# A transformer decoder layer: the quantised feed-forward restructured, and the last batch of the attention layers kept in one piece

## The reference

```python
def _act_fake_quant(x, clip_factor):
    scale = jax.nn.sigmoid(clip_factor) * jnp.max(jnp.abs(x)) / QMAX
    return jnp.clip(_ste_round(x / scale), -QMAX - 1.0, QMAX) * scale
...
xq = _act_fake_quant(x, clip_x[0])
gate = jnp.einsum('bsh,ih->bsi', xq, _weight_fake_quant(w_gate))
up = jnp.einsum('bsh,ih->bsi', xq, _weight_fake_quant(w_up))
h = _act_fake_quant(jax.nn.silu(gate) * up, clip_down[0])
return jnp.einsum('bsi,hi->bsh', h, _weight_fake_quant(w_down))
```

## Time and profile before

| | |
|---|---|
| median of 3 runs | 1102.18 us (1100.94 to 1102.88) |
| the profiled execution's own time | 1098.88 us |
| its span in the profile | 1097.1 us |
| busy in the span: PE | 917.2 us (84%) |
| DVE | 734.1 us (67%) |
| ACT | 628.8 us (57%) |
| POOL | 355.2 us (32%) |
| mean granted TensorE clock | 0.921 of full speed |

### The profile page before, as it was taken

The page is one execution under the profiler, slowest core; times in us unless marked ns, Lnnn a source line. Parts: engine busy times, 40 slices in busy tenths (PEclk is TensorE's granted clock), DMA queues, the critical chain, the costliest instruction groups (busy, mean ns, idle before and its releaser), DMA issues. The chain is left out here.

```text
span 1097.1 us, 17747 instructions
## 1 busy us (share of the span) xinstructions
PE 917.2 (84%) x5861; PEld 439.7 (40%) x5865; DVE 734.1 (67%) x1566; ACT 628.8 (57%) x1173; POOL 355.2 (32%) x381
## 2 busy tenths in 40 slices
PE   2898999999999997999999887899986884458454
PEld 1443334554445353444453643333443443123222
DVE  6588876677776548786763666878744665376574
ACT  1335777567686733577867345576562443488562
POOL 6821156205311173143025643111033210134223
PEclk9989999999999998999999999999997677688667
DMA  4341172201311321122123113211123112111043
GB/s 146 100 119 51 59 87 64 60 30 52 99 58 39 116 77 57 40 75 90 32 73 107 49 59 98 91 61 45 54 78 113 55 50 80 55 57 58 0 153 115
DMA packets 82600, 79.60 MB, mean 73 GB/s; under 512 B 19560, under 2 KB 76008, under 8 KB 82520
## 3 DMA queue, kind: packets, MB, share of 16 engines
q1 hardware_dynamic: 77384, 75.03, 22.2%
q10 hardware_dynamic: 3456, 2.94, 0.8%
q0 software_dynamic: 1680, 0.58, 0.6%
HBM read 23.48 MB, written 14.18 MB: 34 GB/s over the span
## 5 line engine op out<-in xcount | busy, mean ns | idle before, releaser
L672 ACT ACTIVATE probs<-psum 128x512 f32<-128x512 f32 (+1 forms) x608 | 312.8, 579 | 157.4 <-PE psum L862 154.4
L1027 DVE CUSTOM_DVE_ANT_0 junk<-psum,mask 128x640 bf16<-128x640 f32 (+3 forms) x256 | 252.5, 1022 | 60.6 <-PE psum L827 58.7
L592 POOL TENSOR_SCALAR_AFFINE_SELECT probs<-probs 128x512 f32<-128x512 f32 x128 | 82.2, 645 | 372.2 <-ACT probs L672 372.1
L862 PE MATMUL psum<-q_stack,k_stack 98*128 98x512 bf16 (+3 forms) x768 | 186.8, 331 | 14.7 <-ACT probs L672 5.5
L887 PE MATMUL psum<-probs,v_sb 128*17 128x512 f32 (+3 forms) x1536 | 158.8, 493 | 1.8 <-POOL probs L592 1.6
L827 PE MATMUL psum<-k_stack,q_stack 96*128 96x512 bf16 (+3 forms) x512 | 130.1, 349 | 12.9 <-DVE rowmax L1027 9.1
L862 PEld LDWEIGHTS psum<-q_stack,k_stack 98*128 98x128 bf16 x768 | 62.1, 97 | 149.8 <-ACT probs L672 95.1
L1023 DVE TENSOR_REDUCE rowmax<-psum 128x4 f32<-128x512 f32 (+2 forms) x96 | 97.1, 1044 | 35.5 <-PE psum L821 35.3
L787 PE MATMUL psum<-xnT,wT 128*128 128x512 f32 x192 | 94.3, 625 | 0.4 <-ACT probs L672 0.3
L714 PE MATMUL psum<-wT,xnT 128*128 128x256 f32 x384 | 89.3, 390 | 1.7 <-ACT xnT L640 1.5
L677 ACT ACTIVATE xprobs<-psum 77x512 f32<-77x512 f32 x128 | 67.6, 590 | 29.0 <-PE psum L871 28.7
(11 more groups left out here) (152 smaller groups left out, 1310.0 us busy)
## 6 DMA issues: line engine op xcount, KB each, us to landing
k_stack<-k_parts SPq DMA_DIRECT2D x216, 64.0 KB, 2.6
q_stack<-q_parts SPq DMA_DIRECT2D x192, 64.0 KB, 2.6
xq_stack<-xq_parts SPq DMA_DIRECT2D x192, 64.0 KB, 2.6
xn<-in_x SPq DMA_DIRECT2D x8, 512.0 KB, 6.3
res<-in_x SPq DMA_DIRECT2D x4, 1024.0 KB, 6.4
resid_hbm<-res SPq DMA_DIRECT2D x8, 512.0 KB, 2.6
normT_hbm<-xnT SPq DMA_DIRECT2D x8, 512.0 KB, 7.1
xf<-normT_hbm SPq DMA_DIRECT2D x8, 512.0 KB, 4.2
```

The lines of the kernel that those rows point to most:

```text
L592: nc.gpsimd.affine_select(out=tile, in_=tile, compare_op=ALU.is_ge, fill=0.0, base=0, pattern=[[0, GH], [1, P]], channel_multiplier=-1).th ...
L672: nc.scalar.activation(probs[n % 2][:, heads * k:heads * k + heads, 0:cols], bank_a(s)[:, 0:heads * cols].rearrange("p (h n) -> p h n", h= ...
L862: last = nc.tensor.matmul(bank[:, cols * n:cols * n + cols], k_stack[:, slot, h, P * j:P * j + P], q_stack[:, slot, half, h, q0 - HALF * h ...
L1027: nc.vector.tensor_tensor_reduce(out=junk[D_STEPS.place(s) % 2][:, 0:keys], in0=bank_d(s)[:, 0:keys], in1=m.mask[:, T - keys:T], scale=1.0 ...
```

## The change

**The layers.** The last batch is no longer split: parts(b) gives (BOTH,) for all batches, and lane y is empty. The last batch has no tstore; the tile xnT, which holds its feed-forward input, now lives on into the feed-forward. PICKS is new throughout. In it the query and key projections of batches 2 and 3 stand ahead of the last softmax steps of the batch before (at most 33 and 30 softmax steps follow the first of them); in the old one they stand behind the last of them.

**The feed-forward.** All loops are unrolled, and the last batch's two blocks come first, read from xnT.

- partition_all_reduce is gone. TensorE turns the column of maxima into a row (a transpose), VectorE reduces the row, and TensorE spreads the result (a product with ones).
- GpSimd rounds x (one instruction of 128x1024), three blocks ahead of the tiles.
- All tiles have 128 rows (the weights are padded with zeros). VectorE multiplies tiles 0 to 2, GpSimd tiles 3 to 5, whose up ScalarE copies out.
- VectorE takes one maximum a block over 3072 elements, one block behind; the last block's in two pieces.
- ScalarE rounds a whole block of hidden values in one instruction (3072 elements) and takes the constant off four of the six slices in a second; VectorE takes it off the other two, and clips the block in one instruction, 3072 elements, with both bounds.
- The down projection has four pairs of banks, and its loop over hidden tiles is outside the one over token tiles.

```diff
 def parts(b):
-    return (0, 1) if b == B - 1 else (BOTH,)
+    return (BOTH,)
...
-        s += [("xT", 2, b, c, half) for c in range(CC)] + [("tstore", b, half)]
+        s += [("xT", 2, b, c, half) for c in range(CC)] + ([("tstore", b, half)] if b + 1 < B else [])
...
+    BLOCKS = [NB - 2, NB - 1] + list(range(NB - 2))
+    DEEP = 3
+    MINE, BACK = 3, 4
...
-            nc.gpsimd.partition_all_reduce(small[:, XALL], m.xmax[:], P, RMAX).then_inc(reduced, 1)
...
+            def round_x(n):
+                if n >= 2:
+                    pool.wait_ge(xf_in[n % DEEP], 16 * len([k for k in range(2, n + 1) if k % DEEP == n % DEEP]))
+                    pool.wait_ge(x_cut, n - 1)
+                nc.gpsimd.tensor_scalar(xr[n % 2][:], block_input(n), small[:, XINV], MAGIC, ALU.mult,
+                                        ALU.add).then_inc(x_rounded, 1)
+
+            pool.wait_ge(x_scaled, 1)
+            for n in range(3):
+                round_x(n)
+            for n in range(NB):
+                if n + 3 < NB:
+                    round_x(n + 3)
+                for i in range(MINE, FT):
+                    pool.wait_ge(silu_done, FT * n + i + 1)
+                    nc.gpsimd.tensor_tensor(hidden[:, n, i, :], up[i - MINE][:], silu[i][:], ALU.mult).then_inc(theirs_done, 1)
...
+            for n in range(NB):
+                if n >= 2:
+                    act.wait_ge(hq_dve, n - 1)
+                nc.scalar.activation(hr[n % 2], hidden[:, n, :, :], ACT.Identity, scale=small[:, HINV],
+                                     bias=magic[:, 0:1]).then_inc(h_rounded, 1)
+                act.wait_ge(h_rounded, n + 1)
+                if n >= 2:
+                    act.wait_ge(down_done, n - 1)
+                nc.scalar.activation(hq[n % 2][:, 0:BACK, :], hr[n % 2][:, 0:BACK, :], ACT.Identity,
+                                     bias=magic[:, 1:2]).then_inc(hq_act, 1)
...
+            def over_partitions(column, n):
+
+                nc.tensor.transpose(m.psum[0:1, 0, 0:P], column, m.ident[:]).then_inc(row_full, 1)
+                pe.wait_ge(row_max, n + 1)
+                nc.tensor.matmul(m.psum[:, 1, 0:1], m.ones[0:1, :], small[0:1, TOP], start=True, stop=True).then_inc(spread, 1)
...
+            def cut_x(n):
+                dve.wait_ge(x_rounded, n + 1)
+                if n >= 3:
+                    dve.wait_ge(gu_full, FT * (n - 2))
+                nc.vector.tensor_scalar(xq[n % 3][:], xr[n % 2][:], -MAGIC, QMAX, ALU.add, ALU.min).then_inc(x_cut, 1)
+                dve.wait_ge(x_cut, n + 1)
+                nc.vector.tensor_scalar(xq[n % 3][:], xq[n % 3][:], -QMAX - 1.0, None, ALU.max).then_inc(xq_done, 1)
...
+            for n in range(NB):
+                if n == NB - 1:
+                    largest(n - 1)
+                products(n)
+                if 0 < n < NB - 1:
+                    largest(n - 1)
+                if n + 3 < NB:
+                    cut_x(n + 3)
+            largest(NB - 1, slice(0, MINE))
+            largest(NB - 1, slice(MINE, FT), NB)
...
+            def cut_h(n):
+                here = hq[n % 2]
+                dve.wait_ge(h_rounded, n + 1)
+                if n >= 2:
+                    dve.wait_ge(down_done, n - 1)
+                nc.vector.tensor_scalar(here[:, BACK:FT, :], hr[n % 2][:, BACK:FT, :], -MAGIC, None, ALU.add).then_inc(hq_dve, 1)
+                dve.wait_ge(hq_dve, n + 1)
+                dve.wait_ge(hq_act, n + 1)
+                nc.vector.tensor_scalar(here[:], here[:], QMAX, -QMAX - 1.0, ALU.min, ALU.max).then_inc(hq_done, 1)
```

More of the change, by code:

```diff
@@ new lines, in _ @@
+            act.wait_ge(x_scaled, 1)
+            for n in range(NB):
+                for i in range(FT):
+                    t = FT * n + i
+                    act.wait_ge(gu_full, t + 1)
+                    if n and i < MINE:
+                        act.wait_ge(mine_done, MINE * (n - 1) + i + 1)
+                    elif n:
+                        act.wait_ge(theirs_done, (FT - MINE) * (n - 1) + i - MINE + 1)
+                    last = nc.scalar.activation(silu[i][:], tile_banks[:, t % 4, 0, :], ACT.Silu, scale=gscale[:, i:i + 1])
+                    if i >= MINE:
+                        last = nc.scalar.activation(up[i - MINE][:], tile_banks[:, t % 4, 1, :], ACT.Copy,
+                                                    scale=uscale[:, i:i + 1])
+                    last.then_inc(silu_done, 1)
@@ new lines, in _ @@
+            over_partitions(m.xmax[:], 0)
+            for n in range(NB):
+                pe.wait_ge(xq_done, n + 1)
+                for i in range(FT):
+                    t = FT * n + i
+                    if t < 4:
+                        pe.wait_ge(x_scaled, 1)
+                    else:
+                        pe.wait_ge(silu_done, t - 3)
+                        if (t - 4) % FT < MINE:
+                            pe.wait_ge(mine_done, MINE * ((t - 4) // FT) + (t - 4) % FT + 1)
+                    for half, wt in enumerate((m.wgT, m.wuT)):
+                        for c in range(CC):
+                            last = nc.tensor.matmul(tile_banks[:, t % 4, half, :], wt[:, c, P * i:P * i + P],
+                                                    xq[n % 3][:, c, :], start=(c == 0), stop=(c == CC - 1))
+                    last.then_inc(gu_full, 1)
@@ new lines, in products, with largest @@
+            def products(n):
+                for i in range(MINE):
+                    t = FT * n + i
+                    dve.wait_ge(silu_done, t + 1)
+                    nc.vector.scalar_tensor_tensor(out=hidden[:, n, i, :], in0=tile_banks[:, t % 4, 1, :],
+                                                   scalar=uscale[:, i:i + 1], in1=silu[i][:], op0=ALU.mult,
+                                                   op1=ALU.mult).then_inc(mine_done, 1)
+            def largest(n, tiles=slice(0, FT), column=None):
+                dve.wait_ge(mine_done, MINE * (n + 1))
+                if tiles.stop > MINE:
+                    dve.wait_ge(theirs_done, (FT - MINE) * (n + 1))
+                column = n if column is None else column
+                link(nc.vector.tensor_reduce(hmax[:, column:column + 1], hidden[:, n, tiles, :], AX.XY, ALU.max,
+                                             apply_absolute_value=True))
```

315 lines of the change are left out of this document (118 added, 197 removed).

## The result

The changed kernel took 1052.08 us in the median (1050.69 to 1059.1, 4 runs), the kernel before 1101.75: a ratio of 0.9564 [0.9521, 0.9607]. Predicted were 1056 us and a range of 1032 to 1080. Two more sets of runs of it gave 1052.6 and 1052.87. The execution profiled first took 1059.1, 1.7 above its span of 1057.4 and 7.0 above the median.

The account below looks back on a forecast made before the run. It took short exchanges to bound the feed-forward and TensorE the layers. Feed-forward 39 us less and layers 7 less took 1097.1 to a 1051 us span, 1056 us in the median, range 1032 to 1080.

Parts of the forecast that it names:

- Changes 1 and 4: Feed-forward's two scales: replacing partition_all_reduce takes the scale of x from 8.7 to 3.6 us, the second from 5.0 to 2.0.
- Change 2: From the scale of x to the first product: 9.4 us becomes 8.0, including 1.2 of waiting behind GpSimd's rounding.
- Change 3: Gate and up tiles: 74.6 us becomes 59.5, VectorE longest at 8.0 a block with a 1.3 shared-port wait.
- Change 5: Rounding and down projection: 70.7 us becomes 54.2, with ScalarE's wide instructions setting 5.2 us a block.
- The 2 us allowed for TensorE's clock: Last stage: allowance for TensorE pausing in each block and its clock falling; 2 us, bounds 0 and 17.
- Change 6, first and second term: Layers before the last softmax product: 9.3 us less from work moved behind it, 8 less idle from earlier projections.
- third term: Last softmax product to feed-forward, 104.8 us before: work returns and cover is lost, +10 us (-10 to +35).
- Rival B: Last batch's chain stands bare, TensorE waits at half clock: third term +35 in place of +10, 1081 us; chance 0.13.
- A: Feed-forward: VectorE and GpSimd block each other throughout, cuts waiting 2.5 us a block; 1071 us; chance 0.13 together with E.
- D: Layers, 100 to 820 us: new order lowers TensorE's clock by a tenth, costing 70 us; 1126 us; chance 0.06.
- E: Last stage: wide instructions gain nothing and it stays at 70 us; 1072 us; chance 0.13 together with A.
- C: Layers: the order is the better part, second term 20 us and third 0; 1034 us; chance 0.13 for this or more.

Follow-up runs that it names:

- e4: The changed kernel with partition_all_reduce on GpSimd back for both scales; 1068.8 us, 0.9716 of the kernel before.
- e6: The changed kernel with the rounding of x moved from GpSimd to ScalarE, still wide; 1049.77 us, 0.9539 of the kernel before.
- e8: The changed kernel with VectorE's last products ahead of the maximum of the block before; 1047.47 us, 0.9527 of the kernel before.
- e5: The changed kernel with ScalarE's last-stage rounding and constant removal in 512-element instructions again; 1065.09 us, 0.9686 of the kernel before.
- e2: The new feed-forward behind the old layers (old order, last batch split, its store kept); 1058.69 us, 0.9638 of the kernel before.
- e3: The new layers ahead of the old feed-forward, the last batch's store kept; 1098.02 us, 0.997 of the kernel before.
- e9: The changed kernel with the last batch's transposed attention output in the values' buffer instead of xnT; 1048.57 us, 0.9531 of the kernel before.
- e11: The changed kernel with last products first, x rounded on ScalarE and the transposed output in the values' buffer; 1043.93 us, 0.9488 of the kernel before.
- e1: The changed kernel measured again, unedited; 1052.6 us, 0.9571 of the kernel before.
- e7: The changed kernel with two products a block on VectorE and four on GpSimd, in place of three each; 1052.81 us, 0.9573 of the kernel before.

## Why the prediction was right, point by point

- **Changes 1 and 4, the scales.** 3.5 and 2.0 us against 3.6 and 2.0. e4 shows that the removed instruction's cost lay mostly around it, and sizes what the prediction had only as the 17.37 us before GpSimd's first product: the next instruction on GpSimd starts 5.1 us later.
- **Change 2, to the first product.** 7.3 against 8.0. GpSimd's first rounding takes 1.1 us (1.2 was taken), a later one 1.57 beside VectorE's cuts. The wait of the first block's second cut is 0.72 us (1.15 against 0.43), not 1.2, since the rounding of block 1 had been under way for 0.8 us when the cut began. By the Trainium skill (SBUF — State Buffer, Who interferes with whom), as the prediction gave it, the lock holds in both directions and leaves a reduction alone: the trace agrees, with 1.57 us for a rounding beside a cut and 3.33 to 3.35 for every maximum of 3072, whatever GpSimd does beside it.
- **Change 3, the tiles.** 59.8 against 59.5, with VectorE the fullest, a set of products every 7.5 us in the middle (7 to 8 was said), the maximum 3.34 against 3.4. The port wait is the term that a trace of the kernel before could only hint at the earlier trace rows: 1.2 us a block in the five blocks where 1.3 was taken. e6 shows that it is real and in part on the path: taking away 4.8 us of waits gave 1.9. The sign "some cuts over 1.5 us" did not come in the tiles, where the longest took 1.38; only the last stage has such cuts (2.49 and 2.79). That the total is right to 0.3 us is luck. VectorE's eight sets of products start at 942.96, 949.19, 956.94, 964.47, 972.00, 979.08, 984.44 and 993.95 us. The four steps from the second set to the sixth took 29.9 us where the sum has 4 x 8.0 = 32.0; from the seventh set to the end it was 18.4 us where the sum has 16.2 (2.2 and 3.4 for each of two sets and maxima, 3.7 and 1.3), since the maximum ahead of the last products held up everything behind it. By e8 that placing cost 3.9 us, which the sum had nowhere. How the 14.8 us that this stage gained divide among its many edits (the wide maximum, GpSimd's and VectorE's shares, the unrolled loops), no run shows.
- **Change 5, the last stage.** 52.6 against 54.2. ScalarE's pair takes 4.87 and not 5.2: its second instruction starts 0.03 us behind the first, and the next block's overlaps its end, so there were next to no hand-overs: eight pairs are 39.0 us and not 41.6. From the last pair's end to TensorE's last block it was 1.9 us and not 1.0, since the last clip ran beside GpSimd's addition. The 2 us allowed for TensorE's clock were not needed while ScalarE ran beside it: after the first block (4.7 us) none took over 4.52 us, less than ScalarE's 4.87. It was close, though. The 4.3 us taken from the earlier trace rows is no value at half clock; in e5 one block took 5.41, longer than ScalarE's pair here. By the Trainium skill (TensorE: Matmul & The Clock Gate, Part 1), as the prediction gave it, short pauses leave the clock up. The trace does not agree: with pauses of at most 2.4 us between blocks the clock was low again from the third block on in every second block (0.61 to 0.66 there), stayed low in the last, and was 0.73 over the stage. The same Part of the Trainium skill also tells of a kernel in which frequent short idles between groups of matmuls made the clock swing between its levels; this stage looks like that one, and the prediction left it out. It costs nothing while ScalarE is slower still, and 1.5 us in the last block.
- **Change 6, first and second term.** Said: 17.3 less before the last softmax product, 806.6 us. The first profile has 805.4; over the nine profiles of these layers with the new feed-forward (all but e2, e3, e9 and e11) the mean is 801.4, 22.5 less. TensorE's busy time up to that product fell from 748.8 us to 741.8 (737.0 in the mean of nine), 7 to 12 us for the first term's 9.3; its idle time fell from 75.1 to 63.6 (64.4), about 11 us for the second term's 8. So the second was too small by about 3, if idle time is put down to the order alone; no run parts the two.
- **Change 6, third term: the term that was mis-sized.** "I take +10": it was +22 in the first profile and +18.4 over nine, within the bounds given (-10 to +35). The rows of TensorE's groups from the last softmax product to the feed-forward show what grew. First the kernel before:

```profile
L714 PE MATMUL psum<-wT,xnT 128*128 128x256 f32 x48 | 14.1, 458 | 1.5 <-ACT xnT L640 1.5
...
L775 PE MATMUL psum<-ident,xn 128*128 128x128 f32 x40 | 8.1, 369 | 7.2 <-DVE xn L956 6.8 <-DVE xn L1051 0.4
...
L775 PE MATMUL psum<-ident,y_nat 128*128 128x128 f32 x8 | 1.1, 280 | 0.8 <-DVE y_nat L1051 0.8
```

Then the changed kernel (first profile):

```profile
L714 PE MATMUL psum<-wT,xnT 128*128 128x256 f32 x64 | 16.7, 427 | 0.0
...
L775 PE MATMUL psum<-ident,xn 128*128 128x128 f32 x48 | 11.0, 424 | 17.7 <-DVE xn L956 16.5 <-DVE xn L1051 1.2
...
L746 PE MATMUL psum<-identb,k_parts 128*128 128x128 bf16 (+1 forms) x24 | 2.8, 257 | 7.5 <-DVE k_parts L986 7.5
L775 PE MATMUL psum<-ident,y_nat 128*128 128x128 f32 x16 | 2.6, 315 | 5.6 <-ACT xnT L640 4.5 <-DVE y_nat L1051 1.2
```

The work that came back is 5.5 us of TensorE's busy time (77.8 to 83.3; 2.7 in the mean of nine), under the 9.3 said. Its idle time rose from 27.0 to 43.5 (42.8 in the mean): 10.5 more before the transposes of a normalised batch, 7 more before the transposes of the weights' parts that VectorE makes, 4.8 more before those of y, and less elsewhere. So the loss of cover, named but priced at next to nothing, was the larger part. It has three sources. Lines of the changed kernel show the first two:

```profile
826.02 2.70 DVE L938 BATCH_NORM_STATS2 stats<-res 128x6 f32<-128x256 f32 x8
...
833.08 3.67 PE L775 MATMUL psum<-ident,xn 128*128 128x128 f32 x16 [8.24 <-DVE xn L956]
...
834.39 4.53 POOL L587 TENSOR_TENSOR res<-res,bias_f 128x2048 f32<-128x2048 f32 x1 [20.06 <-DVE xn L956]
...
835.74 3.20 DVE L981 TENSOR_SCALAR wscale<-wscale 128x5 f32<-128x5 f32 x1
```

The largest is VectorE's normalisation of the whole batch, eight tiles of statistics and then the chain to the first normalised tile, through which TensorE now stands 8.24 us at one of the two norms and about as long at the other; the prediction counted this chain only as a saving (one of two). The second is VectorE's quantisation of the weights, beside GpSimd's work on the whole batch: a step on 128x5 numbers, 0.17 us later on, takes 3.20 beside the bias addition of 4.53 us, and the steps behind it stretch beside GpSimd's splitting of the queries (L986 0.495 us on average, 0.293 before). That this is the port again is argued, no run took it away. The third is the store that still read xnT, which e9 shows. Rival B was right in kind: of the 25 us from +10 to +35 the first profile went 12, the mean 8; the clock of the stretch, 0.72, was as low before (0.71).
- **The sum.** The feed-forward gained 43.2 us in the profile and 43.6 in e2, against 39 said; the layers 4.2 in e3 (6.1 by e2 and e1), against 7. The first was 4 us better than said, the second 1 to 3 worse, a small net of two larger errors: in the mean of nine profiles the gain ahead of the last softmax product was 5 us larger than said, the loss behind it 8 us larger; against the medians (49.7 us between them) the forecast came out 4 us high. The span came out the other way, 1057.4 against 1051: the 3.3 us from the profiled execution to the median were read from a single execution, and here the profiled one lay 7.0 above its median. Rivals A, D and E did not occur: the cuts of the five later blocks wait 1.2 us a block and not 2.5, the clock of 100 to 700 us is 0.98 (0.99 before), and e5 prices the width. C was right in that the second term was larger than said, about 11 and not 20, but not that the third is nothing.

## What to carry to other kernels

Where many short instructions feed one engine, price the wide form by extending the line through two lengths in the trace; here that was good to 2% at six times the length (3.34 us for 3.41, 2.93 for 2.97) and to 5% at four times (2.00 for 2.10). Before merging a split batch, list for each step of the tail what ran beside it, how long its own chain on another engine is, and which buffer it writes: the cover is the price, more than the work that moves. When VectorE and GpSimd both have work in a loop, count the waits for their port, and look at who else could take GpSimd's share before moving more to it (e6 against e7).

## What the runs showed of the hardware that was not expected

- GpSimd stood 8.74 us before and 6.91 us behind a partition_all_reduce of 0.38 us (e4), so the instruction is paid on both sides.
- A VectorE step on 128x5 numbers that takes 0.17 us alone took 3.20 us beside a GpSimd addition of 4.53 us.
- TensorE's clock alternated between neighbouring blocks for most of the last stage, 0.61 and 1.00 for the same 24 products, with pauses of at most 2.4 us between them.
- The same instructions of the layers ended anywhere from 918.7 to 932.2 us in nine profiles, while the unchanged feed-forward's own 125.1 to 125.4 us (four profiles) hardly moved. The stretch of the last batch tends to be longer where its clock is lower: 126.8 us at 0.72, 124.8 at 0.74, 122.5 and 119.6 at 0.77. A change of 5 us in the layers can be read only from a stretch of the profile, not from a few times.
